# Shared experts beside the routing, expert weights split a layer earlier, and rows as the stationary operand in the last expert layer

## The reference, cut to what matters

```python
# last block: 16 routed experts (4 per token) and 2 shared ones, hidden width 128
tidx, tw = _route(x, router_weight, e_bias)      # sigmoid scores, 2 of 4 groups, top 4, weights
h = silu(einsum('th,eih->tei', x, gate_w)) * einsum('th,eih->tei', x, up_w)
yo = einsum('tei,ehi->teh', h, down_w)
combine = zeros((T, E)).at[arange(T)[:, None], tidx].add(tw)
routed = einsum('te,teh->th', combine, yo)
shared = (silu(x @ sh_gate_w.T) * (x @ sh_up_w.T)) @ sh_down_w.T
x = x + tanh(g_ffn[1]) * (routed + shared)       # of the normalised x
```

## Time and profile before

| | |
|---|---|
| median of three runs | 2136.8 us (2133.99 to 2139.59) |
| the profiled execution | 2136.91 us |
| its span, first to last instruction | 2135.1 us |
| busy: PE, DVE, ACT, POOL | 1612.1, 1153.7, 900.7, 852.5 us |
| mean granted TensorE clock | 0.89 of full speed |

### The profile page before, as it was taken

The page is one execution under the profiler, slowest core; times in us unless marked ns, Lnnn a source line. Parts: engine busy times, 40 slices in busy tenths (PEclk is TensorE's granted clock), DMA queues, the critical chain, the costliest instruction groups (busy, mean ns, idle before and its releaser), DMA issues. The chain is left out here.

```text
span 2135.1 us, 44594 instructions
## 1 busy us (share of the span) xinstructions
PE 1612.1 (76%) x16536; PEld 1221.2 (57%) x16536; DVE 1153.7 (54%) x2584; ACT 900.7 (42%) x1524; POOL 852.5 (40%) x1085
## 2 busy tenths in 40 slices
PE   0699998550699999999980059999962349999997
PEld 0456664450688888888870035666532336666654
DVE  3478887360455555555543446777736462224457
ACT  0477776220444444444430036766543313333332
POOL 0055555266000000000006627777623777215633
PEclk9899999755899999999995579999985569999999
DMA  3343432332444245544102243333212359979985
GB/s 100 80 75 76 73 71 39 145 124 93 145 151 151 84 142 151 151 97 134 36 31 76 81 94 68 71 73 73 56 52 79 136 150 257 198 168 248 235 200 160
DMA packets 385523, 246.94 MB, mean 116 GB/s; under 512 B 318383, under 2 KB 361179, under 8 KB 383656
## 3 DMA queue, kind: packets, MB, share of 16 engines
q1 hardware_dynamic: 359080, 158.81, 31.5%
q0 software_dynamic: 26240, 85.32, 13.2%
HBM read 70.64 MB, written 100.66 MB: 80 GB/s over the span
## 5 line engine op out<-in xcount | busy, mean ns | idle before, releaser
L1174 PE MATMUL ps<-m_xT,m_w_halves 128*128 128x256 f16 x3360 | 414.8, 274 | 67.3 <-DVE m_w_halves L1231 67.3
L1174 PEld LDWEIGHTS ps<-m_xT,m_w_halves 128*128 128x128 f16 x3360 | 329.8, 98 | 106.8 <-issue 67.4
L1534 PE MATMUL ps<-m_routedT,m_w_halves 128*128 128x128 f16 (+1 forms) x2496 | 265.6, 239 | 29.4 <-DVE m_tile_expert L1763 8.2
L601 ACT ACTIVATE a_probs<-ps 128x1024 f32<-128x1024 f32 (+1 forms) x256 | 234.5, 916 | 109.3 <-PE ps L485 106.6
L1534 PEld LDWEIGHTS ps<-m_routedT,m_w_halves 128*128 (+1 forms) x2496 | 182.0, 98 | 115.9 <-issue 64.9
L1152 POOL DMA_DIRECT2D expert_out<-m_y x40 | 28.8, 721 | 536.3 <-DVE m_y L1239 536.3
L1189 PE MATMUL ps<-m_w_halves,m_hiddenT 128*128 128x256 f16 x1680 | 229.3, 273 | 8.4 <-DVE m_hiddenT L1250 8.4
L702 POOL TENSOR_TENSOR a_probs<-a_probs,a_half_above 128x512 f32<-128x512 f32 x128 | 162.2, 1267 | 166.7 <-ACT a_probs L601 166.7
L1221 ACT ACTIVATE m_hiddenT<-m_hidden 128x256 f16<-128x256 f32 x280 | 116.6, 416 | 182.5 <-DVE m_hidden L1247 182.5
L1476 POOL DMA_INDIRECT m_gathered<-routed_out,m_routed_row x128 | 125.3, 979 | 169.7 <-DVE x_res L1786 92.2
L1250 DVE TENSOR_TENSOR m_hiddenT<-m_hidden,m_hiddenT 128x256 f16<-128x256 f32 x280 | 119.2, 426 | 134.9 <-ACT m_hiddenT L1221 134.9
(11 more groups left out here) (247 smaller groups left out, 2827.5 us busy)
## 6 DMA issues: line engine op xcount, KB each, us to landing
routed<-m_zeros POOLq DMA_DIRECT2D x32, 768.0 KB, 4.8
routed_out<-m_y SPq DMA_DIRECT2D x48, 512.0 KB
m_w_load<-in_L_w SPq DMA_DIRECT2D x24, 896.0 KB, 6.8
dispatched<-m_zero SPq DMA_DIRECT2D x10, 1024.0 KB, 13.3
expert_out<-m_y POOLq DMA_DIRECT2D x40, 256.0 KB, 2.7
a_ctx_in<-in_ctx SPq DMA_DIRECT2D x32, 256.0 KB, 2.9
m_w_load<-in_L_experts SPq DMA_DIRECT2D x3, 2304.0 KB, 9.0
x_res<-in_x SPq DMA_DIRECT2D x4, 1024.0 KB, 9.4
```

The source lines that it names most:

```text
L601: A(pr[:, g % 2, 2 * jp:2 * jp + 2, :], SC[:, :, 0:SPAN], ACT.Exp, scale=1.0 / math.sqrt(DH)).then_inc(asem["ex"], 1)
L1174: last = mm(psum[:, v % HB, m * CH:(m + 1) * CH], wh[:, u, ws_, m, d_ * F0 + f_ * P:d_ * F0 + (f_ + 1) * P], xT[:, q % XB, xs_ * KT + d_, ...
L1534: last = mm(psum[:, bank, c0:c1], wh[:, ws_, bass.ds(e, 1), w0:w0 + P].rearrange("p a n -> p (a n)"), xd[:, l % XB, xs_ * KT + d_, c0:c1], ...
```

## The change

**moe0** also loads the 18 experts of moe1 one by one (SP, 384 KB each), splits each into halves (ScalarE and VectorE, one instruction each of 768 elements per partition, at fixed units) and stores the halves to `w16` in DRAM (SP). **moe1** reads them back by five DMAs that ScalarE issues at its start, the shared experts first; its own loads and splits are gone.

The 8 shared jobs run first, two in each batch of the routing, on all engines. `route` becomes `choose`, `place` and `weigh`. The transposes of a batch now go through one PSUM bank in four quarters, and `xn` has two buffers.

In a routed unit the rows are the stationary operand, and gate and up of a tile move together, 256 columns: 24 matmuls. The result has rows on the partitions, so its halves are turned by 8 transposes on TensorE (`turn`) and copied out of PSUM by VectorE (`take_turned`). The down product comes two units later than its hidden product. SP puts the loads first and the store of unit `r` behind the loads of unit `r` + 5. Combinations stand at ten of the late units, and six behind the last.

The dispatched and routed rows are declared as f32 in DRAM (the same bytes) and viewed as f16 by the transposing loads. Semaphores are shared between the two layers with offsets (`R0`, `H0`, `X0`, `GOT0`).

```diff
...
 
-    routed = [nc.dram_tensor(f"routed{b}", (ROUTED, 2 * D), F16, kind="Internal").ap() for b in range(RG)]
+    routed = [nc.dram_tensor(f"routed{b}", (ROUTED, D), F32, kind="Internal").ap() for b in range(RG)]
...
                         pool.indirect_dma_start(disp, bass.IndirectOffsetOnAxis(ap=sidx[:, k, t:t + 1], axis=0),
-                                                xhl[:, t, :, :].rearrange("p s d -> p (s d)"), None, bounds_check=E0 * ROWS - 1, oob_is_err=False)\
+                                                xhl[:, t, :, :].rearrange("p s d -> p (s d)").bitcast(F32), None, bounds_check=E0 * ROWS - 1, oob_is_err=False)\
...
+                def load_next_layer(e):
+                    if e >= 2:
+                        sp.wait_ge(e_lo, e - 1)
+                    sp.dma_start(el[:, e % 2, :], a["L1_experts"][:, e, :]).then_inc(e_in[e % 2], 16)
+
+                def store_next_layer(e):
+                    sp.wait_ge(e_lo, e + 1)
+                    sp.dma_start(w16[:, :, e, :], eh[:, e % 2, :, :]).then_inc(e_sent[e % 2], 16)
...
+                    if q % 2 == 0 and q // 2 < E1:
+                        load_next_layer(q // 2)
+                    if q % 2 == 1 and 3 <= q < 2 * E1 + 3:
+                        store_next_layer((q - 3) // 2)
+                for u in range(2):
+                    sp.wait_ge(e_sent[u], 16 * (E1 // 2))
...
+                def split_next_layer(e):
+                    act.wait_ge(e_in[e % 2], 16 * (e // 2 + 1))
+                    if e >= 2:
+                        act.wait_ge(e_sent[e % 2], 16 * (e // 2))
+                    A(eh[:, e % 2, 0, :], el[:, e % 2, :], ACT.Copy).then_inc(e_hi, 1)
...
+                    if v % (2 * FT) == FT + 4 and v // (2 * FT) < E1:
+                        split_next_layer(v // (2 * FT))
...
+                def split_next_layer(e):
+                    dve.wait_ge(e_hi, e + 1)
+                    V.tensor_tensor(eh[:, e % 2, 1, :], el[:, e % 2, :], eh[:, e % 2, 0, :], ALU.subtract)\
+                     .then_inc(e_lo, 1)
...
+                    if v % (2 * FT) == FT + 5 and v // (2 * FT) < E1:
+                        split_next_layer(v // (2 * FT))
...
-        NL = 3
-        n_ = NE // NL
-        with nc.sbuf_tensor("m1_w_load", [P, n_, WE], F32) as wl:
...
+        R0, H0 = RG, CHUNKS0 * FT0
+        X0 = [16 * 2 * len(range(u, CHUNKS0, XB)) for u in range(XB)]
+        GOT0 = 4 * 64
+        turned = [psum[:, 4 + u, :].bitcast(F16).rearrange("p (s n) -> p s n", s=2) for u in range(2)]
...
+        def gate_and_up(q):
+
+            pair = psum[:, 2 * (q % 2):2 * (q % 2) + 2, :]
+            if q >= NS:
+                parts = pair.rearrange("p b (t m f) -> p (b t) m f", t=2, m=2)
+                return parts[:, :, 0, :], parts[:, :, 1, :]
+            return tuple(pair[:, m, :].rearrange("p (t f) -> p t f", t=QT) for m in range(2))
...
-                for i, c in enumerate(chunks):
-                    if i:
-                        sp.wait_ge(w_lo, i)
-                    sp.dma_start(wl[:, :, :], a["L1_experts"][:, c * n_:(c + 1) * n_, :]).then_inc(w_loaded, 16)
-                sp.wait_ge(w_lo, NL)
...
+                        sp.wait_ge(h_done, H0 + last_unit(l - XB) + 1)
+                    if l < NJ:
+                        sp.wait_ge(x_lo, R0 + l * QT // RT + 1)
+                    elif (l - NJ) % GROUPS == 0:
+                        sp.wait_ge(sent[(l - NJ) // GROUPS], RT * K1 * 16)
+                    for t in range(QT):
+                        if l < NJ:
+                            src = xhl[:, l * QT // RT, l * QT % RT + t, :, :].rearrange("p s d -> p (s d)")
+                        else:
+                            r0 = ((l - NJ) % GROUPS * QT + t) * P
+                            src = routed[(l - NJ) // GROUPS][r0:r0 + P, :].bitcast(F16)
+                        sp.dma_start_transpose(xd[:, u, :, t * P:(t + 1) * P], src).then_inc(x_in[u], 16)
+
+                def store(r):
+                    sp.wait_ge(y_out, 2 * (NJ + r + 1))
+                    r0 = r % GROUPS * CH
+                    sp.dma_start(eo[r // GROUPS][r0:r0 + CH, :].rearrange("(t p) d -> p t d", p=P), y[:, r % YB, :, :])\
+                      .then_inc(y_sent[r % YB], 16)
+
+                for l in range(NJ + NR):
                     load(l)
-                for l in range(NR + NJ):
-                    if l + XB < NR + NJ:
-                        load(l + XB)
-                    if l < NR:
-                        sp.wait_ge(y_out, 2 * (l + 1))
-                        r0 = l % GROUPS * CH
-                        sp.dma_start(eo[l // GROUPS][r0:r0 + CH, :].rearrange("(t p) d -> p t d", p=P),
-                                     y[:, l % YB, :, :]).then_inc(y_sent[l % YB], 16)
+                    if l >= NJ + XB + 2:
+                        store(l - NJ - XB - 2)
+                for r in range(NR - XB - 2, NR):
+                    store(r)
...
+                def shared_hidden(j, i):
+                    q = 2 * j + i
+                    pe.wait_ge(x_in[j % XB], X0[j % XB] + 16 * QT * (j // XB + 1))
+                    pe.wait_ge(w_in[0], 16)
                     if q >= 2:
-                        pe.wait_ge(g_done, q - 1)
+                        pe.wait_ge(g_done, H0 + q - 1)
...
+                def down(l, products):
...
                             pe.wait_ge(y_out, 2 * l - 1 + half)
                         for t in (2 * half, 2 * half + 1):
-                            for i, (q, experts) in enumerate(parts):
-                                e = [e for e, c0, c1 in experts if c0 <= t * P < c1][0]
...
+                                for hs_, ws_ in ((0, 0), (0, 1), (1, 0)):
...
+                                              hT[:, u, hs_, t * P:(t + 1) * P], w2, start=k == 0, stop=k == total - 1)
+                                    k += 1
...
+                def shared_down(j):
+                    pe.wait_ge(hl, H0 + 2 * j + 2)
+                    down(j, [(i, [E1 + i] * QT) for i in range(2)])
...
+                def routed_hidden(r, experts):
+                    l, q = NJ + r, NS + r
+                    pe.wait_ge(x_in[l % XB], X0[l % XB] + 16 * QT * (l // XB + 1))
+                    pe.wait_ge(g_done, H0 + q - 1)
+                    for t in range(QT):
+                        k = 0
+                        for d_ in range(KT):
+                            for xs_, ws_ in ((0, 0), (0, 1), (1, 0)):
+                                both = wh[:, ws_, bass.ds(experts[t], 1), 0:2 * KT * P]\
+                                    .rearrange("p a (m c n) -> p (a m) c n", m=2, c=KT)[:, :, d_, :]
+                                last = mm(psum[:, 2 * (q % 2) + t // 2, t % 2 * 2 * P:(t % 2 + 1) * 2 * P],
+                                          xd[:, l % XB, xs_ * KT + d_, t * P:(t + 1) * P], both,
+                                          start=k == 0, stop=k == 5)
+                                k += 1
+                    last.then_inc(h_done, 1)
+
+                def turn(r):
+                    pe.wait_ge(hl, H0 + NS + r + 1)
+                    if r >= 2:
+                        pe.wait_ge(t_out, r - 1)
+                    for half in range(2):
+                        for t in range(QT):
+                            last = tr(turned[r % 2][:, half, t * P:(t + 1) * P], hm[:, r % 2, half, t * P:(t + 1) * P],
+                                      ident16[:, :])
+                    last.then_inc(t_done, 1)
+
+                def routed_down(r, experts):
+                    pe.wait_ge(t_out, r + 1)
+                    down(NJ + r, [(r % 2, experts)])
+
                 router_logits(0)
-                router_logits(1)
                 for n in range(RG):
+                    shared_hidden(2 * n, 0)
+                    shared_hidden(2 * n, 1)
                     positions(n)
-                    if n + 2 < RG:
-                        router_logits(n + 2)
-                pe.wait_ge(w_lo, NL)
+                    shared_down(2 * n)
+                    shared_hidden(2 * n + 1, 0)
+                    shared_hidden(2 * n + 1, 1)
+                    if n + 1 < RG:
+                        router_logits(n + 1)
+                    shared_down(2 * n + 1)
+                pe.wait_ge(w_in[1], 64)
                 pe.wait_ge(te_ready, RG)
-
...
-                down(NR + NJ - 1, before)
+                experts = {0: experts_of(0)}
+                for r in range(NR):
+                    routed_hidden(r, experts[r])
+                    if r >= 2:
+                        routed_down(r - 2, experts.pop(r - 2))
+                    if r + 1 < NR:
+                        experts[r + 1] = experts_of(r + 1)
+                    if r >= 1:
+                        turn(r - 1)
+                routed_down(NR - 2, experts[NR - 2])
+                turn(NR - 1)
+                routed_down(NR - 1, experts[NR - 1])
...
+                def load_weights():
```

(83 more changed lines are left out.)

276 lines of the change are left out of this document (121 added, 155 removed).

## The result

The changed kernel takes 2171.5 us (median of 4, 2169.5 to 2174.5), the kernel before 2135.4 us (median of 4) beside it: ratio 1.0171, 95% interval 1.0150 to 1.0192, so 36 us slower. A second measurement on another chip gave 2176.6 to 2139.3 us, 1.0168 (1.0141 to 1.0194). Forecast were 2181 us and slower.

The account below looks back on a forecast made before the run. The routed loop was taken as bound equally by TensorE and SP's DMA issue, 6.5 us a unit. Front +72, loop -11 and tail -17 made +44 on a 2135.1 us span: 2181 us executed, range 2134 to 2212, likeliest 2165 to 2197.

Parts of the forecast that it names:

- The loop's limit: Routed loop: SP's DMA issue stays at 6.48 us per unit, so TensorE's lighter unit gains nothing; stretch 11 us shorter.
- The unit: Routed unit on TensorE: products 3.0, turning transposes 0.8, down 1.5, register loads 0.2; 5.5 us for 6.5.
- The turned copy: Routed unit on VectorE: copying 1,024 elements per partition out of PSUM takes 1.23 us, from 0.7 to 1.4.
- The front: Last layer before its first routed matmul: shared experts join the routing chain, passes of 54 us; 72 us longer.
- The doubling: Shared passes in the front: at half clock the columns' part doubles, hidden 2.60 to 5.15 us, down 2.78 to 5.2.
- The tail: After the last down product: only the last gathers remain, 56.8 us instead of 74.2, so 17 us less.
- The first expert layer: Added loads, stores, copies and subtractions for the last layer's weights stay hidden: 0, at most 7 us.
- (a): Rival, routed loop: TensorE sets a faster pace, 5.0 to 5.1 us a unit, 2115 us; chance 0.14.
- (b): Rival, front: it runs at full clock, 25 us less, 2156 us; chance 0.2.
- (c): Rival, front: half clock throughout, 27 us more, 2208 us; chance 0.12.
- (d): Rival, routed loop: turn and copy make VectorE a limit in combining units, ten times 1 to 2 us, 2195; chance 0.07.
- (e): Rival: full clock and no long SP instructions, or a front overlapping more than summed: 2137 us, no change; chance 0.09.

Follow-up runs that it names:

- e12: Changed kernel with ScalarE's queue storing routed results and VectorE taking the next group's lower halves and choice before adding the second shared job: 2120.9 us, ratio 0.9935.
- e7: Kernel before the change, with only the routed results stored by ScalarE's queue instead of SyncE: 2325.0 us, ratio 0.9986.
- e3: Changed kernel leaving out one of three products in the routed hidden product, 16 matmuls a unit for 24: 2310.1 us, ratio 0.9920 to the kernel before.
- e6: Changed kernel with weights stationary again: 48 small products, no turn or copy, down one unit behind hidden: 2353.3 us, ratio 1.0104 to the kernel before.
- e2: Changed kernel with each routed result stored by two half-size DMAs on SyncE: 2328.4 us, ratio 1.0004 to the kernel before.
- e11: Changed kernel without the last layer's shared experts (products, activations, additions): 2079.4 us, ratio 0.9716 to the kernel before.
- e10: Kernel before with last-layer weights split in the first expert layer, rows stationary and ScalarE's stores; shared jobs stay behind routed units: 2090.9 us, ratio 0.9771.

## Why the prediction was right

**The loop's limit.** The step that carried the prediction, that TensorE's lighter unit gives nothing because SP's issue is level with it, held: 6.42 us a set against 6.48 forecast, TensorE waiting 53.5 us for rows, loop 312.5 us against 310. By its terms: first matmul to SP's first load 2.8 us (2.9 forecast), SP's loads and stores 289.5 (290.3), landing and last hidden product 8.1 (4.4 forecast; TensorE still had the unit before in hand), the rest 12.1 (12.4). Removing the stores gave 18 us after (e12), and nothing before, on a chip that starves (e7); removing a third of the hidden products gave at most 0.2 us of 0.9 (e3); adding 1.5 us to TensorE's unit cost 0.3 (e6). One part of the reasoning was too simple: the set is not the sum of its issues. A store taken away gives 0.4 to 0.45 of its 0.62 us, one added costs 0.2 to 0.4 (e2), and without stores more of the transposes are held up: their mean is 1.45 us in e12's loop (6.0 us a set) and 1.39 in the kernel after's, with a median of 1.27 to 1.28 in both. A busy share of the DMA engines near 1 does not explain it alone: in the first expert layer before, at a share of 0.38, 23 of the 80 transposes of the earlier trace rows took over 1.4 us too, 1.43 in the mean. What holds up single transposes was not isolated. The price of a transpose itself, over the whole last layer (ns min/median/max):

```profile
L1473 SPq DMA_TRANSPOSE m_routedT<-routed x192: 1191/1272/2430, 1776.3 to 2093.8; - x192
```

As before the change, none was below 1.19 us.

**The unit.** The 24 products took 2.78 us (forecast 3.0), the turn 0.61 (0.8), down 1.47 (1.5): 4.9 with 5.3 forecast, and 5.5 with register loads. The 0.2 us for these was an estimate, and 4.43 us from turn to turn leave them no time of their own. The turned copy was mis-sized most: 0.68 us against 1.23. The row that I took was a reduction over f32 words; the copy reads and writes two-byte words. It decided nothing, since VectorE had room in most units (busy for 132 of the loop's 312.5 us).

**The front.** +65.6 us against +72. By the marks of the forecast, from the end of the logits: lower halves at +5.9 (7.2), rows landed at +16.9 (16.4), placing at +27.4 (26.9), next logits' end at +53.3 (54) in the second pass and 51.4 in the third; the first pass 43.3 (44); from the last logits to the first routed matmul 44.1 (47.8). From the layer's start the first logits took 21.8 us and not 20.5 (ScalarE's five issues took 3.6 us and not 2.5); the passes were 0.7 to 2.6 us shorter than forecast, and the end 3.7 us. The sum has half clock in the logits and in the first pass behind them and full clock after that, as an estimate from the earlier trace rows, and so it came: logits 7.0 us at a granted clock of 0.50 (1646.92 to 1653.93 us), the first shared pass behind them 7.0 to 7.7 us for its 24 matmuls (7.75 forecast) at 0.69 to 0.76, the next 5.3 to 5.5 (5.2) at 0.97 to 1.00, with 0.69 over the front. The doubling held too: inside the first of these passes the matmuls of 512 columns start 0.42 us apart at 0.50 (six from 1614.2 to 1616.3 us) and 0.22 us apart at 1.00 (13 from 1618.2 to 1620.8). That was right for this order of work only; e12 has the same passes at 5.35 us. The stream of the first expert layer began at 549.07 us, so its window at 0.50 lies two to five us in. ScalarE's table loads took 1.28 us each, two a pass. e11 shows the term in the whole: 101 us is what the shared jobs add, and 35 us (148.3 to 113.1) is what the rest of the new front gives back. The split weights with the old routing gave 40.8 us in e10, so they account for all of it, and the new order of the routing gives nothing by itself. The forecast had this only as a net.

**The tail.** 55.9 us against 56.8, -18.2 against -17. The shared jobs left the tail, and the last 32 gathers with their last combination remained, in e11 and e12 too (55.9 and 56.4).

**The first expert layer.** Nothing lost, as forecast: the last layer began at 1588.8 us, at 1593.3 in the repetition and 1591.6 before, which is the scatter of the layers ahead of it.

**The rivals.** (a), TensorE sets the pace: refuted; its price of 5.0 to 5.1 us a unit was fair (4.9, and 4.43 from turn to turn), but no transpose fell to the 1.15 us that it needed (the least 1.19). (b) and (c), clocks: between the two, as taken. (d), VectorE: not a limit, but the loop's waits do name it, which the forecast had set down as a sign of being wrong. Of the 10.5 us, 4.6 lie behind the last hidden product, where the forecast had the copies in its sum; the other 5.9 us are five waits inside the loop. SP waited 2.9 us for TensorE after its first load, so they can have cost the loads no more. (e) did not come. The sum of the terms was 8 us high: 6 in the front, 3 by the layer's earlier start and 1 in the tail, less 2 in the loop.

## What to carry to other kernels

When two limits lie level, here 6.5 us of TensorE and 6.5 us of DMA issue, a lighter unit on one is worth only what the other leaves; count the queue that issues DMAs as an engine, instruction by instruction. Work moved to "fill" an idle engine costs the length of the chain that it joins, not its own time: 81 us of products made the routing 101 us longer, while at the end of the layer they hid the gathers. Before a step is put behind another in an engine's order, look up what it really needs: the lower halves needed nothing of the job that they stood behind, and with the choice moved ahead of it the front was 33 us shorter.

## What was unexpected of the hardware

- On chips A and B the engines starved while GpSimd issued indirect DMAs. In e7 TensorE got 1 or 2 matmuls every 1.4 us, about one indirect DMA's time (0.97 us and a gap of 0.30); from 1780 to 1840 us VectorE and ScalarE did nothing, and ScalarE once waited 97.9 us. The kernel before took 190 us more there. The cause was not found.
- A VectorE copy of 1,024 two-byte words per partition out of PSUM takes 0.68 us, as long as a product over 512 words of f32 (0.69 us).
- ScalarE's queue issues a store of 512 rows in 0.37 us (median of 48 in e7, 0.366 to 0.435), SyncE in 0.58 us.
